# A four-layer transformer kernel: mixture stage with gates by DMA and expert sums on GpSimd, a written-out store program, and regions closed without a GpSimd drain

## What is computed

```python
x = x + _L0_attn_ref(_layernorm(x), ...)   # linear attention, then a mixture of 4 experts
x = x + _L0_ffn_ref(_layernorm(x), ...)    # one of 8 experts for each token, 256 hidden
x = x + _L1_attn_ref(_layernorm(x), ...)   # softmax attention over 512 tokens
x = x + _L1_ffn_ref(_layernorm(x), ...)    # one of 8 experts for each token, 512 hidden

# in _L0_attn_ref, the mixture:
gw = jax.nn.softmax(jnp.einsum('btd,ed->bte', h, w_moe_gate), axis=-1)
hid = jax.nn.silu(jnp.einsum('btd,efd->btef', h, w1) + b1)      # 4 experts x 512 hidden
eo = jnp.einsum('btef,edf->bted', hid, w2) + b2
ffn = jnp.einsum('bte,bted->btd', gw, eo)
# in _L0_ffn_ref, the choice and its weight:
gate_probs = jax.nn.softmax(gate_logits, axis=-1)
top_val = jnp.max(gate_probs, axis=-1)
top_val = top_val / (top_val + 1e-08)
```

## Time and profile before

| what | us |
| --- | --- |
| median of 3 executions (1525.73 to 1536.03) | 1526.29 |
| the profiled execution, its own time | 1526.64 |
| its span, first to last instruction | 1524.8 |
| PE busy in the span | 1296.3 (85%) |
| DVE busy | 1003.6 (66%) |
| ACT busy | 801.9 (53%) |
| POOL busy | 689.2 (45%) |
| attention_front | about 8.8 to 472.8 |
| mixture | 472.8 to 956.2, first matmul at 486.3 |
| routed(0) | 956.2 to 1086.0 |
| softmax_attention | 1086.0 to 1354.7 |
| routed(1) | 1354.7 to 1524.8 |

### The profile page before, as it was taken

One profiled execution on the slowest core, in us unless ns is written; L12 is line 12 of the kernel. 1 busy time (PEld: TensorE's weight loads), 2 busy tenths in 40 slices (PEclk: granted clock), 3 DMA queues, 4 the chain that ended last, 5 costly groups with the idle time before them and its releaser, 6 DMA issues. The chain is left out here.

```text
span 1524.8 us, 34022 instructions
## 1 busy us (share of the span) xinstructions
PE 1296.3 (85%) x10546; PEld 1013.7 (66%) x10546; DVE 1003.6 (66%) x3454; ACT 801.9 (53%) x1647; POOL 689.2 (45%) x845
## 2 busy tenths in 40 slices
PE   3899999999983999999999992667399999749996
PEld 1566666666652888888888881556277776539996
DVE  3677878787844788888888884456467777512221
ACT  2344444444423766666666660455266666525553
POOL 2344444444420044353444535223557788426665
PEclk9999999999975999999999996899699999969998
DMA  2231313131103000000000001556401112169881
GB/s 76 35 42 23 41 21 41 21 41 21 28 2 83 1 8 16 7 14 7 7 14 7 14 8 43 148 168 179 137 25 56 56 58 61 43 230 314 261 259 35
DMA packets 61579, 101.02 MB, mean 66 GB/s; under 512 B 9698, under 2 KB 36331, under 8 KB 61120
## 3 DMA queue, kind: packets, MB, share of 16 engines
q1 hardware_dynamic: 51648, 78.58, 20.1%
q0 software_dynamic: 9856, 21.52, 4.6%
HBM read 62.96 MB, written 29.75 MB: 61 GB/s over the span
## 5 line engine op out<-in xcount | busy, mean ns | idle before, releaser
L1138 DVE TENSOR_TENSOR m_Sl<-m_S,m_Sh 128x512 fp32r<-128x512 f32 x256 | 175.0, 693 | 32.5 <-ACT m_S L1050 27.6
L1050 ACT ACTIVATE m_S<-PS,W 128x512 f32<-128x512 f32 x256 | 175.3, 685 | 33.6 <-PE PS L958 30.5
L1413 POOL DMA_INDIRECT rows<-r_row,r_posi x128 | 139.7, 1091 | 37.4 <-issue 37.3
L1399 POOL TENSOR_TENSOR r_soft<-r_euler,r_soft 128x32 f32<-128x32 f32 x16 | 86.8, 5427 | 133.0 <-DVE r_soft L1295 133.0
L1045 ACT ACTIVATE m_Sh<-PS,W 128x512 fp32r<-128x512 f32 x128 | 88.1, 689 | 105.9 <-PE PS L958 105.6
L751 DVE TENSOR_TENSOR am<-PS,C 128x512 f32<-128x512 f32 x192 | 119.4, 676 | 20.5 <-PE PS L443 20.5
L956 PE MATMUL PS<-m_HH,m_w1h 128*128 128x512 f32 x256 | 110.8, 433 | 14.2 <-DVE m_HL L1102 14.0
L1631 PEld LDWEIGHTS PS<-f_wt,f_hid 128*128 128x128 f32 x960 | 119.6, 192 | 4.0
L1631 PE MATMUL PS<-f_wt,f_hid 128*128 128x128 f32 x960 | 120.0, 276 | 0.0
L1620 PE MATMUL PS<-f_xT,f_wt 128*128 128x256 f32 x480 | 119.6, 387 | 0.0
L344 POOL TENSOR_TENSOR am<-am,C 128x512 f32<-128x512 f32 x64 | 81.3, 1271 | 78.1 <-ACT am L624 78.1
(11 more groups left out here) (245 smaller groups left out, 3222.1 us busy)
## 6 DMA issues: line engine op xcount, KB each, us to landing
f_wt<-wr SPq DMA_DIRECT2D x40, 578.0 KB, 4.6
f_row<-rows SPq DMA_DIRECT2D x40, 260.0 KB, 2.9
f_wt<-wr SPq DMA_DIRECT2D x40, 256.0 KB, 2.9
f_row<-rows SPq DMA_DIRECT2D x40, 132.0 KB, 2.1
mid<-f_res SPq DMA_DIRECT2D x40, 128.0 KB, 2.7
rows<-r_padding SPq DMA_DIRECT2D x16, 260.0 KB, 3.3
X<-x SPq DMA_DIRECT2D x16, 256.0 KB, 5.4
qr<-qphi SPq DMA_DIRECT2D x64, 64.0 KB
```

What stands on the lines that cost most here:

```text
L1050: nc.scalar.activation(S[:, n % 3, :], PS[:, n % 3, :], ACT.Silu, bias=w("b1")[:, n:n + 1]).then_inc(s_ready, 1)
L1138: nc.vector.tensor_tensor(Sl[:, n % 4, :], S[:, n % 3, :], Sh[:, n % 4, :].bitcast(F32), ALU.subtract).then_inc(sl_ready, 1)
L1413: nc.gpsimd.indirect_dma_start(out=self.rows, out_offset=bass.IndirectOffsetOnAxis(ap=self.posi[:, u, t:t + 1], axis=0), in_=self.row[:, u ...
```

## The change

In the regions: every `nc.Block()` becomes `nc.Block(no_gpsimd_drain=True)`, and the two meetings in `clear_semaphores` use semaphores only. At the end of `pool_end` POOL waits in addition for its own last `told`.

In `mixture`: the first weights are loaded at the end of SP's program in `attention_front`, in four pieces; the second in four pieces at the region's start. ACT rounds a piece, DVE subtracts it, piece by piece, seven of the eight pairs between the chunks of batch 0. The gates are transposed once (`gates`, two transposes), stored to `gates` in DRAM, and for each batch one DMA of SP reads them back spread over all 128 partitions into `gb` (4 x 512 columns, two buffers, the second in the memory of the raw second weights); `gp`, `spread` and the constant `sel` (512 columns of the constants) are gone. `oe` has a slot for each expert and two for the first, and POOL adds the four outputs (`sums`), three 512-column additions in a batch; PE transposes the sum only. DVE rounds one chunk in four instead of two in four (`ROUNDED`). The routing has two row buffers, and its transposes, scores, pick and exponential move from the step of p to that of r. `pool_exp` is gone; ACT computes silu of y and of -y instead (y = logit - 1 - largest), whose quotient is minus e to the y.

The padding at the end of a routing is split: SP writes half, ACT the other half. In `routed(0)` SP's program is written out for 40 slots, and results are stored in pairs of slots, by one DMA each.

```diff
 def clear_semaphores(nc):
-    nc.all_engine_barrier()
+    nc.all_engine_barrier(sem_only=True)
...
             stages(sp, steps)
+            for q in range(MOE):
+                sp.dma_start(raw1[:, q * SEQ:(q + 1) * SEQ], w1t[:, q * SEQ:(q + 1) * SEQ]).then_inc(w1_in[q], 16)
...
-        ROUNDED = (1, 3)
-        SPREAD = (3, 6, 9, 14)
+        ROUNDED = (3,)
...
         @block.sync
         def _(sp):
-            sp.dma_start(raw1[:, :], w1t).then_inc(w1_in, 16)
-            sp.dma_start(raw2[:, :], w2t).then_inc(w2_in, 16)
+            for q in range(MOE):
+                sp.dma_start(raw2[:, q * SEQ:(q + 1) * SEQ], w2t[:, q * SEQ:(q + 1) * SEQ]).then_inc(w2_in[q], 16)
+            sp.wait_ge(gT_ready, 1)
+            sp.dma_start(gates_dram.rearrange("(h e) t p -> (e t) h p", h=2), gT[:, :, :]).then_inc(gates_out, 16)
+            sp.wait_ge(gates_out, 16)
+
+            def one(b, v, p, r, tp, tr):
+                if b is not None:
+                    if isinstance(b, int) and b == 1:
+                        sp.wait_ge(w_split, 2 * MOE)
+                    if not isinstance(b, int) or b >= 2:
+                        sp.wait_ge(oe_ready, MOE * (b + (-1)))
+                    src = gates_dram[:, bass.ds(b * CT, CT), :].rearrange("e t p -> e (t p)").unsqueeze(0)
+                    sp.dma_start(gb[v][:, :, :], src.to_broadcast([P, MOE, SEQ])).then_inc(gb_in[v], 16)
+            over_batches(sp, one)
             routing.sp_padding(sp)
...
+            def sums(b, e, v):
+                pool.wait_ge(oe_ready, MOE * b + e + 1)
+                if e > 1:
+                    pool.wait_ge(summed, 3 * b + e - 1)
+                acc = oe[:, total_of(v), :]
+                nc.gpsimd.tensor_tensor(acc, acc, oe[:, e, :], ALU.add).then_inc(summed, 1)
+
-            def one(b, v, p, r):
-                route(routing.pool_scatter, pool, r)
-                route(routing.pool_inverse_deviation, pool, p)
-                route(routing.pool_exp, pool, p)
+            def one(b, v, p, r, tp, tr):
+                if p is not None:
+                    sums(p, 2, 1 - v)
+                    sums(p, 3, 1 - v)
+                route(routing.pool_inverse_deviation, pool, p, 1 - v, tp)
+                if b is not None:
+                    sums(b, 1, v)
+                route(routing.pool_scatter, pool, r, v, tr)
...
         @block.tensor
...
+                    if n == 0:
+                        route(routing.pe_turn, pe, r, v, tr)
+                    if n == 3:
+                        route(routing.pe_scores, pe, r, v, tr)
+                    if n == 7 and p is not None:
+                        back(p, 1 - v)
+                    if n == 8:
+                        route(routing.pe_count, pe, r, v, tr)
...
         @block.vector
...
+                    if n == 3:
+                        route(routing.dve_largest, dve, r, v, tr)
+                    if n == 4 and more:
+                        split_first(b + 1, 1 - v)
+                    if n == 5:
+                        route(routing.dve_pick, dve, r, v, tr)
+                    if n == 6 and more:
+                        split_second(b + 1, 1 - v)
+                    if n == 8 and p is not None:
+                        residual(p)
+                    if n == 9:
+                        route(routing.dve_statistics, dve, p, 1 - v, tp)
+                    if n == 10:
+                        route(routing.dve_place, dve, r, v, tr)
+                    if n == 12:
+                        route(routing.dve_gate, dve, r, v, tr)
+                    if n == 13:
+                        route(routing.dve_normalise, dve, p, 1 - v, tp)
...
+    def act_exp(self, act, b, u, turn):
+        act.wait_ge(self.soft_ready, b + 1)
+        self.nc.scalar.activation(self.soft[:, 1, :, :], self.soft[:, 0, :, :], ACT.Silu)
+        self.nc.scalar.activation(self.soft[:, 2, :, :], self.soft[:, 0, :, :], ACT.Silu, scale=-1.0).then_inc(self.exp_ready, 1)
...
+        self.pad(sp, range(0, EXPERTS // 2))
+
+    def pad(self, eng, experts):
...
             if layer:
...
+                for s in range(NSLOT):
+                    load(s, s % DEPTH)
+                    if s >= DEPTH and s % 2:
+                        store_pair(s - DEPTH - 1, (s - 1) % DEPTH)
```

More of the change, by code:

```diff
@@ L824, in _, with mixture @@
             stages(dve, steps)
-def mixture(nc, sems, X, w, c, PS, before, ones, minus_half, eps, scratch, H, LG, w1t, w2t, rows, slot_row, slot_expert, where, scattered):
+def mixture(nc, sems, X, w, c, PS, before, ones, minus_half, eps, scratch, H, LG, raw1, w1_in, gates_dram, w2t, rows, slot_row, slot_expert, where, scattered):
     with ExitStack() as ctx:
@@ L943, in _ @@
         def _(pe):
-            pe.wait_ge(w_split, 3)
+            first = lambda b: isinstance(b, int) and b == 0
             def up(b, v, n):
@@ L966, in down @@
                 f = slice(n * P, (n + 1) * P)
+                if first(b) and k == 0:
+                    pe.wait_ge(w_split, 2 * e + 2)
                 wait_high(pe, b, n)
@@ L1004, in _, with gates, one @@
-            beside = {11: routing.pe_turn, 13: routing.pe_scores}
-            def one(b, v, p, r):
+            def gates():
+                pe.wait_ge(gates_ready, 1)
+                for h in range(2):
+                    mm = nc.tensor.transpose(PS[:, 6, h * P:(h + 1) * P],
+                                             gate[:, 2 * h:2 * h + 2, :].rearrange("p e t -> p (e t)"), ident)
+                mm.then_inc(gT_psum, 1)
+            def one(b, v, p, r, tp, tr):
                 for n in range(N):
-                    if n == 0:
-                        route(routing.pe_count, pe, r)
@@ L1106, in gated @@
[L1106 to L1124 removed]
+            nc.vector.tensor_tensor(gate[:, :, :], gate[:, :, :], wide(top[:, :]), ALU.mult).then_inc(gates_ready, 1)
@@ L1288, in dve_pick @@
         ins.then_inc(self.pick, 1)
-        wait_apart(dve, nc, self.pick, picks * b + 1, self.scratch)
+        if not self.layer:
+            wait_apart(dve, nc, self.pick, picks * b + 1, self.scratch)
+            nc.vector.scalar_tensor_tensor(self.soft[:, 0, :, :], self.lg[:, :, :], 1.0, self.top[:, :, 0:1].to_broadcast(wide),
+                                           ALU.subtract, ALU.subtract).then_inc(self.soft_ready, 1)
+    def dve_pick(self, dve, b, u, turn):
+        nc = self.nc
+        picks = 3
+        wide = [P, CT, EXPERTS]
+        if self.layer:
+            wait_apart(dve, nc, self.pick, picks * b + 1, self.scratch)
+        else:
+            wait_apart(dve, nc, self.soft_ready, b + 1, self.scratch)
         for t in range(CT):
@@ L1556, in _, with load @@
         def _(sp):
-            def store(s, u):
-                sp.wait_ge(res_ready, s + 1)
-                sp.dma_start(dest[bass.ds(s * SLOT, SLOT), :].rearrange("(p a) d -> p a d", a=2), res[:, u, :, :]).then_inc(stored[u], 16)
-            def step(s, u, turn):
-                if not layer and since(s, DEPTH):
-                    store(s - DEPTH if isinstance(s, int) else s + (-DEPTH), u)
+            def load(s, u):
                 r = sp.value_load(slot_row[0:1, bass.ds(s, 1)], min_val=0, max_val=ROWS - SLOT)
                 e = sp.value_load(slot_expert[0:1, bass.ds(s, 1)], min_val=0, max_val=EXPERTS - 1)
-                if layer and since(s, DEPTH):
+                if since(s, DEPTH):
                     sp.wait_ge(res_ready, s - (DEPTH - 1))
```

286 lines of the change are left out of this document (132 added, 154 removed).

## The result

The changed kernel takes 1471.22 us (median of 4 executions, 1470.24 to 1475.15), the kernel before 1527.01 beside it (4 executions, 1525.73 to 1536.03). The ratio is 0.9639, 95% interval 0.9618 to 0.9661. The direction was right; the forecast was 1450 and the range ended at 1471. The profiled execution took 1471.58 us of its own, its span is 1469.8. So 55.0 us of span were saved where the sum had 75.9.

The account below looks back on a forecast made before the run. TensorE was taken to bound the mixture before (27.06 us a batch), VectorE after. Savings of 1.0 + 9.5 + 30 + 8.5 + 17 + 3.3 + 6.6 = 75.9 from 1526.3 gave 1450 us, range 1434 to 1471.

Parts of the forecast that it names:

- The loop: Mixture's sixteen batches: period from 27.06 to 25.2 us with VectorE the bound, 30 us saved.
- a sum's hold: Mixture loop: each of GpSimd's three sums blocks VectorE for 1.0 us, from a range of 0 to 1.13.
- TensorE bound (24.4): Rival for the mixture loop: TensorE stays the bound, period 24.4 us, time about 1438; chance 0.17.
- The longer hold: Rival for the mixture loop: sums hold VectorE longer, at 1.6 us each the loop gives nothing, 1480; chance 0.14 (1459 to 1480).
- My bound of 25.9 for the loop: Slow bound of the mixture's period, 22.0 + 3.4 + 0.5 us a batch, 18 us saved.
- Mixture's end: Last product, paddings, scatter and POOL DRAIN after the mixture's batches: 8.5 us saved (6 to 10).
- Restart 28 us after the last `m_Sl` matmul, not 36: Expected sign at the mixture's end: the next stage restarts after 28 us instead of 36.
- Softmax stage: End of the softmax stage: SyncE's eight paddings split in two, 3.3 us saved.
- First routed layer: Row loads, one store for two slots: first to last load 97.5 us instead of 114.0, 17 saved (12 to 18).
- First matmul: Start of the mixture: about 3.3 us in place of 13.98 before TensorE's first matmul, 10.5 saved.
- that last term: Very end of the kernel: the 6.59 us DRAIN goes, 6.6 saved, 0 if the program's own close waits as long.
- The front: Set-up: constants shrink from 1092 to 836 KB, about 1.0 us saved.

Follow-up runs that it names:

- e5: Changed kernel with the ring of SiLU results S and the up-projection banks four deep instead of three, sums still on GpSimd: 1462.22 us.
- e13: Changed kernel with rings of four and VectorE's gate step at chunk 14 instead of 12, sums still on GpSimd: 1466.26 us.
- e1: Changed kernel with each of GpSimd's three sums cut from 512 columns to 1: 1444.34 us.
- e15: As e13, with each of GpSimd's sums cut to one column: 1463.57 us in one execution, of which only the period, 23.95 us, is used.
- e7: Changed kernel with TensorE's transposes of the normalised rows at chunk 1 instead of 0 and ScalarE's copy at 2 instead of 1: 1470.51 us.
- e10: Changed kernel with only VectorE's gate step moved, to chunk 14 instead of 12: 1471.88 us.
- e11: Changed kernel with rings of four, the three sums on VectorE and TensorE's transposes of rows at chunk 1: 1444.64 us.
- e12: Changed kernel with rings of four, the three sums on VectorE and the gate step at chunk 14 instead of 12: 1438.97 us.
- e8: Changed kernel with all eight paddings on SyncE again in both routings and the first routed layer's SyncE program as before: 1485.23 us.
- e9: Changed kernel with POOL's DRAIN back in every close: 1481.03 us.
- e2: Changed kernel with each of GpSimd's three sums issued a second time into a tile nobody reads: 1502.62 us.

## Why the forecast was right in kind and 21 us short

**The loop (10.6 of the 20.9).** The step that failed is "With VectorE the bound, and its extra work in lumps between chunks, I add 0.2 for waits that do not fit: 25.2". The runs show 1.8 of waits on VectorE in its place (26.01 less 24.22), and the same 1.8 with three sums more. That VectorE with the sums' hold sets the period was right: with three more sums the period grows by as much as VectorE's busy time. What stands ahead of it was near: VectorE's need without the sums 22.0, measured 21.7 to 21.8; TensorE's 24.4, measured 24.33 (23.9 of its own work and 0.4 for the ring boundary, which I had not seen); a sum's hold 1.0, measured 0.81. From these the larger of the two is 24.3, and the period is 26.01. I took the maximum of two nearly equal sums, 24.3 and 24.2, as if the one engine could always work ahead while the other is late. My reading is that the streams are coupled by rings of three or four chunks, and that a hold comes in one piece at a certain place (0.7 on the product at 650.71, 1.3 on the first `Sl` at 658.11): PE, which has no air left, loses there what it never gets back. That is argued and only in part shown: rings of four give 0.41 back (e5), and with the gate step moved too VectorE's idle time falls from 1.8 to 0.65 (e13). Of the 1.68 us between e1 and the changed kernel all is due to the sums: e1 and e15 show that it is gone with them, in two arrangements. It is less than the 2.44 that VectorE's work falls by, because TensorE's 24.33 is reached first. In e13, with rings and gate step loosened, VectorE is plainly the larger (25.06 against PE's 23.95) and the period only 0.65 above it: there maximum plus a little would have been a fair forecast, but the hold had grown. Which of the meetings of PE and DVE takes how much isn't settled: e7 and e10 moved one each, and the period stayed.

**The rivals.** TensorE bound (24.4): only with the sums away, or on VectorE with rings of four and the turn or the gate step moved (e11, e12). The longer hold, 1.6 for each sum, gave 1480: its number was nearer to the truth than the likeliest, but its mechanism wasn't, for the sums are 1.29 (one of three 1.66, since it starts beside an `Sl`) and hold for 0.81. My bound of 25.9 for the loop, 22.0 + 3.4 + 0.5, was too low for the same missing term.

**Mixture's end (3.7).** "Restart 28 us after the last `m_Sl` matmul, not 36" compared two different ends: to the first row load it was 37.9 before, so 8.5 less would be 29.4; it is 33.1. The chain to the known ends became 2.6 shorter (908.12 less 888.49, against 22.2 before), not 3.7. From there to the first row load it takes 13.48 instead of 15.72, 2.2 less, where the other 4.8 of the forecast lay. For the sum took a landing of 2 us, as the last scatter's row showed it. That was the landing behind an issue of 8.45 us that had hidden the transfers. With the issue halved SP waits 5.0 for the landing, the eight paddings and four scatters (1.35 MB) nearly fill the DMA engines, and POOL gets to the close at 918.7, last. e8 puts the split at 0.6 us. What this stage did save comes from the shorter chain and from the DRAIN (3.8 by e9).

**Softmax stage (2.4).** The same step: 3.3 for splitting the paddings, 0.9 measured, and less than 0.1 of it in the stretch that the paddings set: from the ends known to the first row load it took 13.52 before (1342.56 to 1356.08) and takes 13.47. Against e8, which has no DRAIN either, the split is worth 0.6. The other 0.8 come from ahead of it, and no run tried them. The forecast looked at when SP was through the earlier trace rows, not at how full the DMA engines were meanwhile.

**First routed layer (4.4).** Plain steps are 2.22 (921.60 to 941.59, nine steps), as forecast. In the other thirty, 80.99 us with 15 stores, a store costs 1.0 on average (80.99 less 30 x 2.2, by 15), not 0.7: most steps with one take 2.9 to 3.2, two take 3.6 and 4.1. The 256 KB pair takes longer to issue (0.43 instead of 0.36, and once 1.61); the rest of the difference isn't explained. That is 101.0 from first to last load instead of 97.5; inside the bounds of 12 to 18. The undone version measures 113.45.

**Right.** First matmul 3.46 after PE's last work (3.3 forecast, counted from the region's opening, which makes it 2.9), ScalarE as busy as before (18.4 of a batch, 18.5), a single wait for the gates of batch 0 (491.3, 20.6 us after the opening at 470.7; forecast 19 to 22), gate loads hidden in every later batch though they land in 8.0, the transposes of the sum not late within the loop, no DRAIN at the end. 0.9 of that last term went elsewhere in the last layer: from its first row load to the end it takes 168.7 before, 163.0 in the changed kernel and 169.9 with the DRAINs (e9), so without the DRAIN's part it is 1.2 longer than before, for a reason that no run shows. The front gave 1.1 more than forecast; it isn't the DRAINs, by e9, and in e8, whose front is the same, it ends 1.5 later, so the 1.1 may be chance.

## What to carry to other kernels

When work is moved from a full engine to a neighbour until both are equally loaded, the maximum of the two sums is a floor, not a forecast: here two engines at 24.3 and 24.2 gave 26.0. A full row of PE says little: read what the same matmuls take where nothing is late. Count ring slots against the loop's length (3 against 16) and ask at each meeting point what is late there. An addition that VectorE can do in 0.69 us is dearer on GpSimd once VectorE is busy all the time, since it holds VectorE for 0.8 to 1.1. And before a transfer's issue is split over two queues, look at the row of DMA load: where it read 8 and 9 there was little to win, and where it read half the split filled it, but with dearer transfers; it gave 0.6 us in both places, where the forecast had 3.3 and more.

## What the runs showed of the hardware

- The hold works both ways and for one-input instructions too: GpSimd's one-column sum 0.57 instead of 0.19 beside `Sl`, VectorE's cast 1.70 instead of 0.43 beside two sums. The Trainium skill, "SBUF — State Buffer", section "SBUF: two separate sides", says that whichever of the two starts first has the pair for its whole instruction; the one-column sum, which waits for the `Sl` already under way, agrees. By the records' start times the others do not: the cast starts 0.09 before the sums (635.91, 636.00) and the `Sl` at 658.11 starts 0.17 before its sum, and VectorE is the one held both times (that `Sl` alone takes 2.01, the two of its row 2.61). The power that left the cast alone stays unexplained.
- What three sums of 1.3 to 1.7 us cost VectorE depends on what stands beside them: 0.81 each in the changed kernel and in e2, 1.12 in e13.
- One load of 1024 KB spread from DRAM to 128 partitions landed in 8.0 us, a plain load of the same size in 4.9 (a second plain one, issued 0.4 behind it, in 8.0).
- The same 1.35 MB of paddings and scatters took 4.5 us of all 16 DMA engines from one queue beside POOL's and 6.3 from two.
- POOL's DRAIN at the mixture's close takes 5.3 us (949.4 before, 917.1 in e9) though POOL has waited for the landing of its indirect DMAs ahead of it (`pool_end`). At the close of the front, where POOL issues none, it takes 0.3 (e9, 463.6).
